# One unrolled program in place of three blocks: the mLSTM mixer in short steps beside the MLP and beside the feed-forward tiles

## What is computed

```python
x = x + attn(layernorm(x))       # Mamba block, then its gated MLP
#   x' = x + mamba(x);  a, g = split(rms(x') @ fc1_w.T)   (256 -> 2 x 1024)
#   x' + (a * silu(g)) @ fc2_w.T                          (1024 -> 256)
x = x + mlstm(layernorm(x), ctx, ctx)    # 4 heads of 64
#   ig, fg = gates of concat(q, k, v);  cs = cumsum(log_sigmoid(fg))
#   log_D = cs - shifted cs + ig, causal;  D = exp(log_D - rowmax)
#   C = (q k^T / 8) * D;  h = (C / max(|sum C|, exp(-rowmax))) @ v
#   h = normalise each head over its 64 channels, times (1 + out_w)
x = x + ffn(layernorm(x))        # 256 -> 2 x 704 -> 256
#   every operand in fp4 steps: blocks of 16, scale = max|x| / 6
#   q(silu(q(x) @ q(w_gate).T) * (q(x) @ q(w_up).T)) @ q(w_down).T
```

## Time and profile before

| | |
|---|---|
| median of 3 runs | 642.43 us (637.57 to 644.45) |
| the profiled execution | 637.39 us |
| its span, first to last instruction | 635.6 us |
| busy: PE, PE weight load, DVE, ACT, POOL | 575.2, 467.5, 446.2, 269.4, 145.4 us |
| mean granted TensorE clock | 0.957 of full speed |

### The profile page before, as it was taken

One profiled execution on the slowest core, in us unless ns is written; L12 is line 12 of the kernel. 1 busy time (PEld: TensorE's weight loads), 2 busy tenths in 40 slices (PEclk: granted clock), 3 DMA queues, 4 the chain that ended last, 5 costly groups with the idle time before them and its releaser, 6 DMA issues. The chain is left out here.

```text
span 635.6 us, 9620 instructions
## 1 busy us (share of the span) xinstructions
PE 575.2 (91%) x3023; PEld 467.5 (74%) x3023; DVE 446.2 (70%) x968; ACT 269.4 (42%) x562; POOL 145.4 (23%) x208
## 2 busy tenths in 40 slices
PE   6799996789999889999999999789986799999995
PEld 5576663578888777877888889778874477777774
DVE  5885899398984134353454456448898999999995
ACT  3476778776884422121111110164532444444441
POOL 4120010244542110111011010202666322222200
PEclk9799999799999989999999999689975899999999
DMA  8200000000000600000000000133410000000000
GB/s 301 84 2 0 1 13 7 5 7 6 6 3 2 235 1 1 1 1 17 1 17 18 1 17 18 51 92 112 122 45 1 1 9 18 17 17 17 17 17 26
DMA packets 22528, 20.99 MB, mean 33 GB/s; under 512 B 12120, under 2 KB 20696, under 8 KB 22104
## 3 DMA queue, kind: packets, MB, share of 16 engines
q1 hardware_dynamic: 22008, 20.41, 9.9%
q10 hardware_dynamic: 480, 0.07, 0.1%
HBM read 16.04 MB, written 2.34 MB: 29 GB/s over the span
## 5 line engine op out<-in xcount | busy, mean ns | idle before, releaser
L724 PE MATMUL ps<-xnT,w_fc 128*128 128x256 f32 x512 | 114.3, 384 | 0.0
L724 PEld LDWEIGHTS ps<-xnT,w_fc 128*128 128x128 f32 x512 | 97.7, 192 | 13.2
L1496 PE MATMUL ps<-w_fc,scores 128*128 128x352 f32 x256 | 83.7, 482 | 5.6 <-ACT scores L1562 5.6
L1125 DVE TENSOR_TENSOR xs<-ps,xs 128x512 f32<-128x512 f32 x32 | 22.1, 691 | 74.6 <-ACT xs L932 74.6
L1496 PEld LDWEIGHTS ps<-w_fc,scores 128*128 128x128 f32 x256 | 49.4, 198 | 33.2 <-ACT scores L1562 6.5
L932 ACT ACTIVATE xs<-ps 128x512 f32<-128x512 f32 x32 | 19.1, 597 | 108.5 <-PE ps L724 69.9
L737 PE MATMUL ps<-zs,xs 128*128 128x256 f32 x256 | 56.6, 379 | 0.0
L737 PEld LDWEIGHTS ps<-zs,xs 128*128 128x128 f32 x256 | 48.6, 190 | 6.6
L1020 DVE SCALAR_TENSOR_TENSOR fold<-xpad,conv_w,fold 128x256 f32<-128x256 f32 x120 | 50.6, 479 | 0.8
L1514 PE MATMUL ps<-u_res,hT 128*128 128x256 f32 x192 | 44.2, 380 | 3.8 <-DVE scores L1668 2.8
L1514 PEld LDWEIGHTS ps<-u_res,hT 128*128 128x128 f32 x192 | 36.3, 190 | 11.3 <-issue 3.0
(11 more groups left out here) (261 smaller groups left out, 1176.4 us busy)
## 6 DMA issues: line engine op xcount, KB each, us to landing
xs<-in_ctxT SPq DMA_DIRECT2D x16, 256.0 KB, 3.3
zs<-in_ffn_w SPq DMA_DIRECT2D x1, 2112.0 KB, 9.6
x_res<-in_x SPq DMA_DIRECT2D x8, 256.0 KB, 7.6
w_fc<-in_w_fc SPq DMA_DIRECT2D x1, 2048.0 KB, 10.3
xs<-xnT SPq DMA_DIRECT2D x8, 256.0 KB, 3.3
xs<-in_ctx SPq DMA_DIRECT2D x16, 128.0 KB, 2.6
out<-scores SPq DMA_DIRECT2D x16, 128.0 KB, 1.7
fold<-in_w_in SPq DMA_DIRECT2D x2, 580.0 KB, 6.3
```

The costliest lines, as they stand in the source:

```text
L724: last = pe.matmul(bank[half + r][:, i * S:(i + 1) * S], m.w_fc1[:, kk, col:col + P], m.xnT[:, b, kk * S:(kk + 1) * S], start=(kk == 0), s ...
L1125: dve.tensor_tensor(hid[:, p, 2 * pair:2 * pair + 2, :].rearrange("p k t -> p (k t)"), bank[r][:], gate[:, r, :], ALU.mult).then_inc(g["hi ...
L1496: last = pe.matmul(bank[1 + j][:, 0:HALF], xT[:, p, k * P:(k + 1) * P], m.w_gu[:, k, j * HALF:(j + 1) * HALF], start=(k == 0), stop=(k == ...
```

## The change

The three parts become one function, `program`, in one block and with no loops: every instruction is written out, and the gates part is dissolved into it. The Mamba stages (k = 0 to 17) stay as they are. What followed is laid out in 38 slots. In slots 0 to 16 a batch of the MLP takes two slots; in slots 17 to 36 there is no MLP. A feed-forward tile t enters at slot 16 + t: x onto the grid in slot 17 + t, `gate_up` in 18 + t, `product` and hf onto the grid in 19 + t, `down` in 20 + t, `output` in 21 + t.

A mixer batch b opens in slot 13 + 2b and closes in the next one. So batches 0 and 1 lie in slots 13 to 16 beside the MLP, and batches 2 to 7 in slots 17 to 28 beside the feed-forward tiles. Its PSUM use goes from eight banks to two (5 and 6): in an open slot PE writes the arguments of the first row block in two halves (`mix_args0`), ACT takes their exponentials, PE writes the second block's arguments into bank 5 (`mix_args1`) and ACT takes those, then come the first scores; in the closing slot the other scores and the sums. `mix_normalise`, `mix_squares`, `mix_variance` and `mix_scale` of a batch stand in the open slot of the next one. "Open" and "closing" slot are used in this sense below.

The gates' chain (log-sigmoid, scans, maxima) is done in two halves of four batches, in slots 10 and 11 and in slots 18 to 20, on 16 rows of 256 columns each; the gates themselves are computed in row form (four matmuls of 256 columns, in place of eight of 8 columns with 128x128 weights each). The weight transposes lie in slots 7 to 11. `gate_up` is three column pieces of 472 instead of four of 352. The warm-up transposes of the gates part (36) are gone. So are the copies of q by DMA: the scores read q where it is. In SP's queue the loads of a mixer batch (keys, values, maxima) are issued one batch ahead, in slot order, with the store of a finished tile behind them; on POOL the powers and residual sums of mixer, layernorms and tiles stand in slot order as well.

The diff, cut to its core:

```diff
     SCAN, MLP = 9, 18
-    STEPS = MLP + B + 3
+    MIX = 13
+    EARLY = 4
+    FWD = MIX + 3
+    SLOTS = FWD + T + 5
+    opens = lambda slot: (slot - MIX) // 2 if slot >= MIX and (slot - MIX) % 2 == 0 else -1
+    closes = lambda slot: opens(slot - 1)
+    CHAIN = [10, 18]
+    LF_AT, NM_AT, PARTS_AT = 15, 20, 25
     PAD = CONV - 1
     TAPPED = 6
...
+        def mix_args0(b, par):
...
+            after(pe, x["h_read"], b)
+            to = bank[5 + par].rearrange("p (k t) -> p k t", k=2)
+            pe.matmul(to, m.minus_one[:], rows_of_maxima(b)[:, par], start=True, stop=False, skip_group_check=True)
+            pe.matmul(to[:, :, 0:P], m.ident_h[:], middle(m.masked_h[:], 2), start=False, stop=True,
+                      skip_group_check=True).then_inc(x["arg0_ps"], 1)
...
+        def mix_args1(b):
+            pe.wait_ge(x["w0_exp"], 2 * b + 1)
...
+        def mix_scores0(b, par):
+            if par == 0:
+                pe.wait_ge(km_in[b % 2], 16 * (b // 2 + 1))
+                pe.wait_ge(x["w0_exp"], 2 * b + 2)
+                pe.wait_ge(g["qT_ready"], min(6 + b, B))
+            else:
+                pe.wait_ge(x["w1_exp"], b + 1)
...
+        def mix_sums(b, c):
+            p = b % 2
+            pe.wait_ge(x["w_ready"], 3 * b + 2 + c)
+            pe.wait_ge(v_in[p], C * 16 * (b // 2 + 1))
...
-            on(fc1, k - MLP, 2)
-            on(fc1, k - MLP, 3)
-            on(fc2, k - MLP - 1)
-            on(turn_q, k - MLP - 2)
-            on(gates, k - MLP - 3)
+        for slot in range(MLP_SLOTS):
+            j = slot // 2
+            if slot % 2 == 0:
+                on(fc1, j, 0)
+                if slot == 0:
+                    turn(B - 1, 0)
+                    turn(B - 1, 1)
+                    project_out(B - 1, 0)
+                    project_out(B - 1, 1)
+                on(turn_xn, j + 4)
+                on(mix_scores0, closes(slot), 1)
+                on(mix_scores1_even, closes(slot))
+                on(fc2, j - 1, 0)
+                on(turn_weights, 2 * (slot - 7), n=W_GROUPS)
+                on(mix_scores1_odd, closes(slot))
+                on(mix_sums, closes(slot), 0)
+                on(fc2, j - 1, 1)
+                on(turn_weights, 2 * (slot - 7) + 1, n=W_GROUPS)
+                on(mix_sums, closes(slot), 1)
+            else:
+                on(fc1, j, 1)
+                on(turn_weights, 2 * (slot - 7), n=W_GROUPS)
+                on(mix_args0, opens(slot), 0)
+                on(mix_args0, opens(slot), 1)
+                on(fc1, j, 2)
+                on(mix_args1, opens(slot))
+                on(turn_q, j - 1)
+                on(fc1, j, 3)
+                on(turn_weights, 2 * (slot - 7) + 1, n=W_GROUPS)
+                on(mix_scores0, opens(slot), 0)
+                if slot == CHAIN[0] + 1:
+                    turn_rows(0)
+                on(gates, j - 1)
+        for slot in range(MLP_SLOTS, SLOTS):
+            on(turn_out, slot - FWD - 4, range(4, KF), n=T)
+            on(turn_in, slot - FWD - 2, n=T)
+            on(turn_out, slot - FWD - 4, range(4), n=T)
+            on(mix_args0, opens(slot), 0)
+            on(mix_scores0, closes(slot), 1)
+            if slot == MLP_SLOTS:
+                mix_args0(opens(slot), 1)
+                turn_q(B - 1)
+            on(gate_up, slot - FWD - 2, 0, n=T)
+            if slot != MLP_SLOTS:
+                on(mix_args0, opens(slot), 1)
+            on(mix_scores1_even, closes(slot))
+            if slot == CHAIN[1] + 2:
+                turn_rows(1)
+            on(gate_up, slot - FWD - 2, 1, n=T)
+            on(mix_args1, opens(slot))
+            on(mix_scores1_odd, closes(slot))
+            on(mix_sums, closes(slot), 0)
+            if slot == MLP_SLOTS:
+                gates(B - 1)
+            on(gate_up, slot - FWD - 2, 2, n=T)
+            on(mix_scores0, opens(slot), 0)
+            on(mix_sums, closes(slot), 1)
+            on(down, slot - FWD - 4, n=T)
 
     @block.scalar
...
-        mixer = [(scores1_even, 1), (scores0, 1), (scores1_odd, 1), (sums, 2), (args, 0)]
-        forward = [(turn_x, 2), (turn_h, 4), (gate_up, 2), (down, 4)]
-        pipelines(pe, B, mixer, T, forward, BEGIN, OVERLAP)
...
+        for slot in range(MLP_SLOTS, SLOTS):
+            on(turned_in, slot - FWD - 2, n=T)
+            on(turned_out, slot - FWD - 4, n=T)
+            on(mix_exps0, opens(slot), 0)
+            on(mix_exps0, opens(slot), 1)
+            if slot == MLP_SLOTS:
+                turned_q(B - 1)
+            if slot == CHAIN[1]:
+                chain_exp(1)
+            if slot == CHAIN[1] + 2:
+                chain_last_exp(1)
+            on(lift_x, slot - FWD - 1, n=T)
+            on(lift_h, slot - FWD - 3, n=T)
+            on(mix_exps1, opens(slot))
+            on(mix_squares, opens(slot) - 1)
+            on(silu_up, slot - FWD - 2, n=T)
+            on(norm_in, slot - FWD, n=T)
...
-        mixer = [(exps, 0), (squares, 2)]
-        forward = [(turned_x, 2), (turned_h, 4), (lift_x, 1), (lift_h, 3), (silu, 2), (norm, 0)]
-        pipelines(act, B, mixer, T, forward, BEGIN, OVERLAP)
...
+        def mix_variance(b):
+            dve.wait_ge(x["sq_ready"], b + 1)
+            after(dve, x["v_rstd"], b - 1)
+            dve.tensor_reduce(var[:, b % 2, :], sq, AX.X, ALU.add).then_inc(x["v_ready"], 1)
...
-        mixer = [(lambda b, p: weights(b, p, 0), 1), (lambda b, p: weights(b, p, 1), 1), (variance, 3),
-                 (normalise, 2), (scale, 3)]
-        forward = [(product, 3), *first, (tile_stats, 0), (output, 5), (tile_mean, 0), *last]
-        pipelines(dve, B, mixer, T, forward, BEGIN, OVERLAP)
...
+        for slot in range(MLP_SLOTS, SLOTS):
+            if slot == MLP_SLOTS:
+                norm(B - 1)
+            if slot == CHAIN[1]:
+                chain_start(1)
+            on(product, slot - FWD - 3, n=T)
+            on(mix_weights0, closes(slot), 0)
+            on(mix_normalise, opens(slot) - 1)
+            for i in range(3):
+                on(step_x, slot - FWD - 1, i, n=T)
+                on(step_h, slot - FWD - 3, i, n=T)
+            on(mix_weights0, closes(slot), 1)
+            for i in range(3, 5):
+                on(step_x, slot - FWD - 1, i, n=T)
+                on(step_h, slot - FWD - 3, i, n=T)
+            on(mix_weights1, closes(slot))
+            on(mix_variance, opens(slot) - 1)
+            on(tile_stats, slot - FWD, n=T)
+            on(output, slot - FWD - 5, n=T)
+            on(tile_mean, slot - FWD, n=T)
+            if slot == CHAIN[1] + 2:
+                chain_columns(1)
+            if slot == CHAIN[1]:
+                chain_logs(1)
+            if slot == CHAIN[1] + 1:
+                chain_maxima(1)
+            for i in range(6, 9):
+                on(step_x, slot - FWD - 1, i, n=T)
+                on(step_h, slot - FWD - 3, i, n=T)
+            on(mix_scale, opens(slot) - 1)
 
 
```

More of the change, by code:

```diff
@@ L42 @@
 KF = -(-FF // P)
-GU_ROWS = 2 * FF // P
+GU_ROWS = 12
 FFN_W = GU_ROWS * D + KD * FF
@@ L518, in _ @@
+        for each in y_out:
+            sp.wait_ge(each, 16 * (T // 2))
     @block.gpsimd
@@ L578, in _ @@
+        for k in range(MLP):
             on(rstds, 2 * k)
@@ L766, in gates @@
-            last.then_inc(g["gates_ps"], 1)
+            pe.wait_ge(s["xnT_ready"], XN_MOVES)
+            after(pe, g["gates_done"], b // EARLY)
+            for k in range(2 * KD):
+                src = m.xnT[:, b, k * S:(k + 1) * S] if k < KD else kT[:, p, k - KD, :]
+                last = pe.matmul(bank[7][0:3 * ROWS, 0:S], m.gate_pad[:, k, 12 - XH * i:12 - XH * i + 3 * ROWS], src,
+                                 start=(i == 0 and k == 0), stop=(i == EARLY - 1 and k == 2 * KD - 1),
+                                 skip_group_check=True)
@@ L768, in _, with down @@
+        def down(t):
+            pe.wait_ge(f["hT_ready"], t + 1)
+            pe.wait_ge(f["dn_zero"], 1)
+            pe.wait_ge(g["gates_done"], 2)
+            after(pe, f["y_ready"], t)
+            for k in range(KF):
+                last = pe.matmul(bank[7][:, 0:D], hT[:, t % 2, k, :], w_dn[:, k, :], start=(k == 0),
+                                 stop=(k == KF - 1))
+            last.then_inc(f["dn_ps"], 1)
         pe.wait_ge(s["selected"], 1)
         keep_warm(pe, m, 20)
-        for k in range(STEPS):
+        for k in range(MLP):
@@ new lines, in turned_weights @@
+        def turned_weights(n):
+            act.wait_ge(g["w_turned"], n + 1)
+            if n < 6:
+                at = 4 * P * (n // 2)
+                w = min(4 * P, 3 * GU_W - at)
+                last = act.activation(w_gu[:, n % 2, at:at + w], bank[5][:, 0:w], ACT.Copy)
+            else:
+                for k in range(2):
+                    kk = 2 * (n - 6) + k
+                    w = min(P, FF - kk * P)
+                    last = act.activation(w_dn[0:w, kk, :], bank[5][0:w, k * D:(k + 1) * D], ACT.Copy)
+            last.then_inc(g["w_saved"], 1)
```

(29 more changed lines are left out.)

1116 lines of the change are left out of this document (536 added, 580 removed).

## The result

The changed kernel takes 682.41 us (median of 4, 680.74 to 683.98), against 643.44 for the kernel before (4 runs): ratio 1.0638, 95% interval 1.0585 to 1.0691. The forecast was 655, with 674 as the upper end: the sign was right, the size was a third of what came, and the time lies outside the range. The profiled execution took 681.8 with a span of 680.1, 44.5 more than before.

What follows compares the result with a forecast made beforehand. PE was taken to bound the MLP and DVE the feed-forward tiles: 419.7 + 183.9 + 25.8 + 4 + 15.2 = 648.6, 650.4 with 1.8 around the span, and 655 at the runs' median; range 625 to 674 for 8 in 10.

Steps and rivals of the forecast that it cites:

- the wait for the squares: Open slots: DVE's variance waits 2.8 for ACT's squares behind hf's lift and the second exponentials; five slots, 14 in all.
- part one: Up to the end of the last fc2, PE the bound: 395.6 becomes 419.7, bounds 411.7 and 428.
- Turns and gates: Beside the MLP on PE: one more `turn_q` and gates before the last fc2, 1.7.
- The mixer's rows: Beside the MLP on PE: mixer batches 0 and 1 at 5.97 each, less the last sums, 10.2.
- the 8 for waits: Beside the MLP: four new PE waits on other engines, 2 each; bounds 0 and 16.
- slot 17: 7.5: DVE idle in slot 17, waiting for the last fc2, then q's turn and gates: 7.5.
- slot 18: 1.5: DVE idle in slot 18, where tile 0 is alone in the pipeline: 1.5.
- the 4 for the clock: Open slots: PE stretches at half clock after waiting for DVE, mostly hidden by room in the pair, 4 in all.
- part two: Last fc2 to last tile's product, DVE the bound: 183.9 of work, 25.8 idle, plus 4 for PE's clock.
- The sum of a pair: Steady pair of slots: DVE the bound at 25.9, 2.8 of it waiting, against 22.6 of PE's work.
- The rival in which the waits vanish: PE's new waits, variance's wait and half clock mostly go, slot 17 costs as the ramp did: 625 to 629; chance 0.22.
- The rival of the half clock: Open slots: `gate_up` and `down` at half clock after PE's idles make PE the bound of pairs: 672 or 668; chance 0.12.

Runs made afterwards that it cites:

- The experiment with one batch less: Changed kernel with the mixer opening in slot 15, not 13, and tiles two slots later, leaving one batch beside the MLP: 682.1 us.
- Dummies: Changed kernel plus dummy identity transposes where PE idles, behind the last fc2 and in slots 17 to 19: 674.9 us.
- moving the layernorm of q: Kernel with all mends, DVE doing the mixer's normalising before the last q's layernorm in slot 17: 648.6 us, against 653.5.
- the other mends: Changed kernel plus early squares, DVE's order in slots 13 to 16, dummies in slots 17 to 19 and at three places beside the MLP: 653.5 us.
- the dummies in full pairs: Kernel with all mends plus 16 dummy transposes at the end of each of open slots 21, 23, 25, 27: 660.7 us, against 653.5.
- the misplaced dummies: 15 dummy transposes put into slot 9, though the wait stands in slot 11; part of the kernel with all mends, 653.5 us.

## Why the prediction was wrong

What held: the mixer hides nothing under feed-forward tiles, since no engine has room there; a pair of slots (26.57, forecast 25.9), the wait for the squares (2.50, forecast 2.8), the second half chain (11.8 of DVE, forecast 12), the table loads at nothing, the weight transposes (4.2 from start to start), the tail (16.1, forecast 15.2, and 15.1 without the half clock in it).

The step that failed first is the sum of part one, 419.7 with 428 as its upper bound; it was 436.75. Taken from start to start, PE's work in the stage rose by 29.8 for 16.1 forecast; its idle time rose by 9.4, for which the sum had 8; and the MLP started 1.7 later. The work was short in three terms:

- Clock and fc1 and fc2, for which the sum had nothing. The same 768 matmuls took 175.4 in place of 168.4. 5.2 of these 7.0 are clock: four stretches at half clock where the kernel before has one. Slot 0, with the tail of the Mamba block, has a fifth, 1.6.
- Turns and gates rose from 11.5 to 16.2, not by 1.7. Two more sets of gates now lie ahead of the last fc2 and not one; a set with its turn takes 2.1 from start to start, where the sum had subtracted durations, which overlap, and got 1.7; and in row form a set costs 0.15 more.
- The mixer's rows came to 11.9, forecast 10.2.

The bound was wrong too: I let a clock fall stand only behind each new wait, and it fell as well in slot 4, behind a wait that the kernel before has, and behind one of 1.91 for the turn of q, which I had not foreseen. The experiment with one batch less shows the cost of what was moved: some 14 for a batch that the sum had at 5 to 6 and a share of the 8 for waits.

The second is the idle time in slots 17 to 20, the terms "slot 17: 7.5", "slot 18: 1.5" and the 4 for the clock. From 436.75 to the third product DVE was idle for 73.2 − 50.5 = 22.7, where the sum had 11.8 (7.5, 1.5 and a first wait of 2.8) and 4. That is 6.9 of the 13.5 that part two came late; the others are DVE's work (187.2, forecast 183.9) and its idle time behind the third product (17.3, where the sum had 14), in which it also waits 0.93 for scores in each closing slot. I had filled the slots with work by engine; they are a chain of handovers, in which PE at half clock is a link. Dummies took 8.3 out of it; moving the layernorm of q, with the other mends in place, 3.6.

A third step was right by chance. The sum of a pair had DVE as its bound, 23.1 of work and 2.8 of waiting; the dummies in full pairs show PE as the bound at 24.6 without the wait, and DVE's work alone would give 23.1. PE's steps for a batch add up to 7.2 and not to the 5.97 of the earlier trace rows, and what is left of the pair, 24.64 − 7.2 = 17.4, is 8.7 per tile for the 8.30 of the earlier trace rows. The rival in which the waits vanish had 629; with most of the waits mended the kernel is at 648.6. PE's added work stays, by my estimate from these rows some 8 x 1.2 and 14 x 0.4 = 15. That the cutting into short steps raises PE's work fits these rows, but no run undid the cutting alone; it is argued, not shown.

The rival of the half clock had the right mechanism, but its place and price were off. It put it into the steady pairs, where this profile has a clock of 1.00 throughout; it fell in slots 17 to 20 and in five stretches beside the MLP (slots 0, 2, 4, 11 and 16). In other profiles with the same pairs it does fall on `down`, in three pairs at most. The rival counted 3.4 lost per fall, and the rows show 1.7 on PE and 0.9 on a pair.

What stays open: why PE's row is longer when it is cut into short steps, and why the same wait is followed by half clock in one execution and not in another. No version here beats the kernel before; the best, with the 1.6 of the misplaced dummies in it, is 1.1% above it (0.2 to 1.9%).
